# Which groups share the slots of an image, and over how many partitions its transfers run, in a fused group norm, quantised grouped convolution and residual kernel

## What is computed

```
v = group_norm(x, 32 norm groups of 16 channels)          # per image
xg = v by 4 conv groups of 128 channels; output group g reads input group (g + 1) mod 4
xa = round(clip((xg - lA) / (uA - lA), 0, 1) * 15) / 15    # 16 levels
wq = the same for the weights, then (wq - 0.5) * 2         # [4, 128, 128]
y  = per group: wq @ xa                                    # 128 x 128 by 128 x 784
y  = relu(y * inv + (beta - running_mean * inv)),  inv = gamma / sqrt(running_var + eps)
out = x + (y + v)
```

## Time and profile before

| what | us |
|---|---|
| median of 3 runs (317.69 to 323.72) | 322.63 |
| the profiled execution | 316.4 |
| its span | 314.7 |
| busy: PE, DVE, ACT, POOL | 203.8, 232.7, 213.9, 217.8 |
| mean DMA rate over the span | 329 GB/s |
| mean granted TensorE clock | 0.907 of full |

### The profile page before, as it was taken

The page is one execution under the profiler, slowest core; times in us unless marked ns, Lnnn a source line. Parts: engine busy times, 40 slices in busy tenths (PEclk is TensorE's granted clock), DMA queues, the critical chain, the costliest instruction groups (busy, mean ns, idle before and its releaser), DMA issues.

```text
span 314.7 us, 8243 instructions
## 1 busy us (share of the span) xinstructions
PE 203.8 (65%) x3336; PEld 141.0 (45%) x3336; DVE 232.7 (74%) x364; ACT 213.9 (68%) x394; POOL 217.8 (69%) x376
## 2 busy tenths in 40 slices
PE   1122397668586767877777777776858676875640
PEld 0022265455364545455545554554536354643430
DVE  1763567797988979697879897969798796957650
ACT  2222768878797878768797988796978859477000
POOL 5104287787979797959797989797887959696000
PEclk9999999797989989597979997979898698979995
DMA  7999999999999999999999999999999988899987
GB/s 173 231 222 216 215 216 217 270 344 362 398 398 398 398 397 402 401 399 401 395 404 408 411 412 414 408 419 408 409 404 406 404 258 196 187 254 237 244 201 228
DMA packets 19207, 103.56 MB, mean 329 GB/s; under 512 B 2258, under 2 KB 2530, under 8 KB 19170
## 3 DMA queue, kind: packets, MB, share of 16 engines
q1 hardware_dynamic: 10496, 54.86, 53.4%
q10 hardware_dynamic: 8674, 48.18, 44.1%
HBM read 51.65 MB, written 51.38 MB: 327 GB/s over the span
## 4 chain that ended last, share of the span: by engine, by line
PE 44%; DVE 26%; DMA 12%; issue 10%; SPq 3%; ACT 2%; POOL 0%; DVEq 0%; ACTq 0%; POOLq 0%
PE prod L679 39%; DVE images L539 17%; DMA images<-in_x 12%; DVE stats L517 8%; PE mean_ps L638 4%; SPq L222 2%; SPq L234 1%; ACT levels L310 1%; DVE sums L525 1%; ACT unused L274 1%; DVE codes L532 0%; SPq L226 0%; ACT unused L282 0%; DVEq L98 0%; PE var_ps L651 0%
## 5 line engine op out<-in xcount | busy, mean ns | idle before, releaser
L679 PE MATMUL prod<-codes,w_t 64*64 64x392 bf16 x3072 | 165.8, 370 | 51.5 <-DVE images L539 51.5
L539 DVE SCALAR_TENSOR_TENSOR images<-prod,floor,images 128x784 f32<-128x784 f32 x128 | 126.3, 1028 | 50.4 <-PE prod L679 50.3
L679 PEld LDWEIGHTS prod<-codes,w_t 64*64 64x64 bf16 x3072 | 105.0, 119 | 101.9 <-issue 39.2
L470 POOL TENSOR_SCALAR images<-images,coef 128x784 f32<-128x784 f32 x122 | 130.1, 1078 | 0.0
L310 ACT ACTIVATE levels<-images,coef 128x784 int16<-128x784 f32 x95 | 91.4, 1028 | 2.2 <-POOL coef L461 2.2
L517 DVE BATCH_NORM_STATS2 stats<-images 128x6 f32<-128x392 f32 x136 | 66.9, 553 | 17.7 <-DMA images<-in_x 17.7
L274 ACT ACTIVATE unused<-images 128x784 bf16<-128x784 f32 x60 | 50.9, 849 | 40.3 <-DMA images<-in_x 35.8
L282 ACT ACTIVATE unused<-images,sums 128x784 bf16<-128x784 f32 x60 | 56.1, 938 | 0.1
L427 POOL TENSOR_TENSOR dev<-stats,gmean 128x16 f32<-128x16 f32 x16 | 3.7, 229 | 50.6 <-ACT gmean L290 50.6
L532 DVE TENSOR_SCALAR codes<-levels 128x3136 bf16<-128x3136 int16 x32 | 34.1, 1064 | 1.4 <-ACT levels L310 1.4
L481 POOL TENSOR_SCALAR levels<-images,coef 128x784 int16<-128x784 f32 x33 | 33.6, 1020 | 0.1
(11 more groups left out here) (71 smaller groups left out, 83.2 us busy)
## 6 DMA issues: line engine op xcount, KB each, us to landing
images<-in_x SPq DMA_DIRECT2D x60, 784.0 KB, 30.2
out<-images ACTq DMA_DIRECT2D x60, 784.0 KB, 12.5
images<-in_x SPq DMA_DIRECT2D x8, 392.0 KB, 8.1
out<-images SPq DMA_DIRECT2D x2, 784.0 KB, 7.4
out<-images SPq DMA_DIRECT2D x8, 196.0 KB, 3.5
w_raw<-in_weight SPq DMA_DIRECT2D x2, 128.0 KB, 7.4
rows<-in_channel_params ACTq DMA_DIRECT2D x1, 8.0 KB, 1.6
limit_row<-in_limits ACTq DMA_DIRECT2D x1, 0.0 KB
```

The source lines that it names most:

```text
L470: nc.gpsimd.tensor_scalar(here, here, coef[:, u % 2, 0, 1, G * j + o:G * j + o + 1], coef[:, u % 2, 1, 1, G * j + o:G * j + o + 1], ALU.mu ...
L539: nc.vector.scalar_tensor_tensor(out=two, in0=prod[:, PSUM_SET[n % 2][g], :, 0:HALF], scalar=floor[:, o:o + 1], in1=two, op0=ALU.max, op1= ...
L679: done = nc.tensor.matmul(prod[outputs, sets[y], h, 0:HALF], w_t[inputs, part, t, s, outputs], codes[inputs, i % 2, 2 * c + s, h * HALF:(h ...
```

## The change

Groups 0 and 2, and 1 and 3, now share the slots: LOW holds groups 0 (`y = 0`) and 1 (`y = 1`), HIGH holds groups 2 and 3. The views of x, out and the weights are cut by `r` (which half of the partitions, group = 2r + y), so that one transfer takes one `y` with all 128 partitions: in HBM 2 pieces, two groups apart, of 64 rows each. Every load is one transfer per `y`, for the weights too. A store is two transfers, the first after three `final` operations, the second after four. The last image has one transfer per slot. Semaphore counts follow.

The PSUM sets now rotate over all images, (4n + g) mod 3, and `multiply` waits for the `final` operation that frees its second set: three of the image before for t = 0, the first of its own for t = 1, for even and odd images alike. In `multiply` the tiles of output set y read input slots 1 - y, LOW and HIGH from different halves of the partitions; before, all tiles of a set read the same half. The sorting of the weights for it takes 8 operations of 64 partitions instead of 4 of 128. The order of work on the engines is the same, written in another way. Cut to the core:

```diff
-PSUM_SET = ((0, 1, 2, 0), (1, 2, 0, 1))
...
-    GROUPS = ((LOW, slice(0, G, G - 1)), (HIGH, slice(1, G - 1)))
+    HALVES = (LOW, HIGH)
 
     def by_pairs(t):
-        return t.rearrange("b (g i t) h w -> b g i (t h w)", g=G, t=2)
+        return t.rearrange("b (r y i t) h w -> b y r i (t h w)", r=2, y=2, t=2)
 
     x_v, out_v = by_pairs(x), by_pairs(out)
-    w_v = weight.rearrange("(g i t) c -> g i (t c)", g=G, t=2)
+    w_v = weight.rearrange("(r y i t) c -> y r i (t c)", r=2, y=2, t=2)
...
         def store_image(engine, n):
-            engine.wait_ge(final, G * n + G)
-            for part, groups in GROUPS:
-                engine.dma_start(out_v[n, groups].rearrange("y i f -> i y f"),
-                                 pairs_of(images[part, n % RING])).then_inc(stored[n % RING], DMA)
+
+            for y in range(2):
+                engine.wait_ge(final, G * n + 3 + y)
+                engine.dma_start(out_v[n, y], pairs_of(images[:, n % RING])[:, y]).then_inc(stored[n % RING], DMA)
...
-                for part, groups in GROUPS:
-                    sync.dma_start(pairs_of(images[part, j]),
-                                   x_v[n, groups].rearrange("y i f -> i y f")).then_inc(x_loaded[j], DMA)
+                for y in range(2):
+                    sync.dma_start(pairs_of(images[:, j])[:, y], x_v[n, y]).then_inc(x_loaded[j], DMA)
...
-                for part, groups in GROUPS:
-                    sync.dma_start(out_v[B - 1, groups][y][:, t * HW:(t + 1) * HW],
-                                   images[part, j, ORDER[k]]).then_inc(stored[j], DMA)
+                sync.dma_start(out_v[B - 1, y][:, :, t * HW:(t + 1) * HW],
+                               images[:, j, ORDER[k]]).then_inc(stored[j], DMA)
...
-                nc.vector.scalar_tensor_tensor(out=two, in0=prod[:, PSUM_SET[n % 2][g], :, 0:HALF], scalar=floor[:, o:o + 1],
+                nc.vector.scalar_tensor_tensor(out=two, in0=prod[:, (G * n + g) % SETS, :, 0:HALF], scalar=floor[:, o:o + 1],
...
-                done = nc.vector.tensor_scalar(w_sorted[:, g % 2, :, 1 - g // 2], w_rest[:, g].rearrange("p (i s) -> p s i", s=2),
-                                               bn[:, 3, g:g + 1], None, ALU.mult)
+                y, t = g // 2, g % 2
+                for part, inputs in ((LOW, y), (HIGH, 1 - y)):
+                    done = nc.vector.tensor_scalar(w_sorted[part, t, :, inputs],
+                                                   w_rest[part, g].rearrange("p (i s) -> p s i", s=2),
+                                                   bn[part, 3, g:g + 1], None, ALU.mult)
...
-            def multiply(trip, i, t):
-                n, sets = BODY * trip + i, PSUM_SET[i % 2][2 * t:2 * t + 2]
+            def multiply(n, t):
+                first = G * n + 2 * t
                 if t == 0:
                     pe.wait_ge(capped, n + 1)
-                if i > 0 or t == 1:
-                    pe.wait_ge(final, G * n + 1 if t == 1 else G * n - i % 2)
+                if first >= SETS - 1:
+                    pe.wait_ge(final, first + 2 - SETS)
...
-                            for y, inputs in ((0, HIGH), (1, LOW)):
-                                for c, outputs in enumerate((LOW, HIGH)):
-                                    done = nc.tensor.matmul(prod[outputs, sets[y], h, 0:HALF], w_t[inputs, part, t, s, outputs],
-                                                            codes[inputs, i % 2, 2 * c + s, h * HALF:(h + 1) * HALF],
+                            for y in range(2):
+                                for r, outputs in enumerate(HALVES):
+                                    inputs = HALVES[(r + y) % 2]
+                                    done = nc.tensor.matmul(prod[outputs, (first + y) % SETS, h, 0:HALF],
+                                                            w_t[inputs, part, t, s, outputs],
+                                                            codes[inputs, n % 2, 2 * (1 - y) + s, h * HALF:(h + 1) * HALF],
```

More of the change, by code:

```diff
@@ L206, in wait_image @@
             if n < SINGLE:
-                engine.wait_ge(first_loaded[n][g // 2], 2 * DMA)
+                engine.wait_ge(first_loaded[n][g // 2], DMA)
             else:
@@ L220, in _ @@
                 for y in range(2):
-                    for part, groups in GROUPS:
-                        sync.dma_start(pairs_of(images[part, n])[:, y],
-                                       x_v[n, groups][y]).then_inc(first_loaded[n][y], DMA)
+                    sync.dma_start(pairs_of(images[:, n])[:, y], x_v[n, y]).then_inc(first_loaded[n][y], DMA)
                 if n == 0:
-                    for part, groups in GROUPS:
-                        sync.dma_start(pairs_of(w_raw[part]),
-                                       w_v[groups].rearrange("y i f -> i y f")).then_inc(weights_in, DMA)
+                    for y in range(2):
+                        sync.dma_start(pairs_of(w_raw[:])[:, y], w_v[y]).then_inc(weights_in, DMA)
             def load(n):
@@ L244, in _ @@
                 sync.wait_ge(final, G * (B - 1) + k + 1)
-                for part, groups in GROUPS:
-                    sync.dma_start(out_v[B - 1, groups][y][:, t * HW:(t + 1) * HW],
-                                   images[part, j, ORDER[k]]).then_inc(stored[j], DMA)
+                sync.dma_start(out_v[B - 1, y][:, :, t * HW:(t + 1) * HW],
+                               images[:, j, ORDER[k]]).then_inc(stored[j], DMA)
             for j in range(RING):
-                stores = len(range(j, B, RING)) + (G - 1 if j == (B - 1) % RING else 0)
-                sync.wait_ge(stored[j], 2 * DMA * stores)
+                stores = 2 * len(range(j, B, RING)) + (G - 2 if j == (B - 1) % RING else 0)
+                sync.wait_ge(stored[j], DMA * stores)
         @block.scalar
@@ L640, in average_means, with average_deviations @@
                 done.then_inc(mean_done, 1)
[L642 to L643 removed]
+            def average_deviations(u):
                 pe.wait_ge(dev_done, u + 1)
[L645 removed]
+                if u >= 1:
                     pe.wait_ge(std_done, u)
@@ L675, in multiply @@
                             if (part, s, h) == (PARTS - 1, 1, 1):
[L676 to L680 removed]
+                                wait_affines(n, t)
+                            for y in range(2):
+                                for r, outputs in enumerate(HALVES):
[3 more added lines that the diff above has]
+                                                            codes[inputs, n % 2, 2 * (1 - y) + s, h * HALF:(h + 1) * HALF],
                                                             start=(part == 0 and s == 0), stop=(part == PARTS - 1 and s == 1))
                 done.then_inc(multiplied, 1)
[L684 to L690, removed]
             pe.wait_ge(w_scaled, 1)
@@ L696, in _ @@
             turned.then_inc(w_turned, 1)
-            average_means(0, 0)
-            average_deviations(0, 0)
+            average_means(0)
+            average_deviations(0)
             pe.wait_ge(w_ready, 1)
[L700 to L711, removed]
+            average_means(1)
+            for n in range(B):
+                u = n // 2 + 1
+                if n % 2 == 0 and n and u < PAIRS:
+                    average_deviations(u)
+                multiply(n, 0)
+                if n == 0:
+                    average_deviations(1)
+                if n % 2 == 1 and u + 1 < PAIRS:
+                    average_means(u + 1)
+                multiply(n, 1)
 _LIMITS = ["L0_conv_lW", "L0_conv_uW", "L0_conv_lA", "L0_conv_uA"]
```

25 lines of the change are left out of this document (10 added, 15 removed).

## The result

The changed kernel takes 1947.58 us (median of 4 runs, 1947.18 to 1947.69). The kernel before takes 322.17 us beside it (median of 4, 317.69 to 323.72). The ratio is 6.086, with a 95% interval of 6.036 to 6.135. The profiled execution of the changed kernel took 1947.63 us, and 1.7 us of it lie around its span.

A forecast was written before the change was run, and what follows sets the result against it. Two DMA engines at 52.0 GB/s were taken to bound the changed kernel: 1976 us for images, 5 for weights, 2 and 3 at start and end, 1986, with 1.7 around the span 1988, called 1990 us; range 1900 to 2340.

The forecast's parts named there:

- How many engines: Image transfers: outermost counts of 2 and 128 give two DMA engines, 282 packets under 512 bytes; chance 0.86.
- The rate of one engine: Image transfers: 26.0 GB/s for each DMA engine, 52.0 for two, so 1976 us for 32 images both ways.
- The lower bound of 13.6 GB/s with one queue: Stretches of loads or stores alone: each of two engines at only 13.6 GB/s, from 217 / 16 before.
- the high end of 2330: Two engines, slower with one queue: six images of loads and six of stores at 27.2 GB/s, 709 us not 371.
- The start and the pace: First L539 operation at about 163 us and not 42.7, then an image every 62 us.
- Rotation of the sets: Multiply of even images waits for one final less: 0 to 0.85 us for each of 15, some 13; here 0.
- The tile order: Products: even at twice 2.18 us for 48, four groups are 17 us of 61.8, hidden under transfers: 0.
- The half-image stores: First half stored after three final operations: 0 to -1 us per image, counted 0.
- The sorting of the weights: Eight operations, not four of 0.9 us in all: 0 to 1.1 us more, once, during image 1's wait; counted 0.
- The two that kept sixteen engines at a similar or better time: Rivals on transfers: 16 engines, mixed rate also for loads alone, 279 us (0.09); single queue stays at 217 GB/s, 308 to 316 (0.02).
- The 279 us that I gave it: Rival of 16 faster engines: 316.4 less 10 at the start, 23 in the pairs, 4 at the end; chance 0.09.
- The one of slow products: Rival on TensorE: 16 engines, but 48 products take about 4.3 us and not 2.18, some 395 us; chance 0.03.

The follow-up runs named there:

- p1: No computation, transfers alone in 16 forms (pieces in HBM, halves or whole, one or two queues), output copied input: 869.36 us in all.
- e2: The kernel before with the product sets rotating over all images as the only edit: 308.57 us, ratio 0.960.
- e1: The changed kernel with only its transfers undone, each cut by half of the partitions again: 305.47 us, ratio 0.954.
- e7: e1 with each half of an image stored early, in two transfers of 64 partitions, four per image: 304.39 us.
- e6: e5 with its stores changed likewise: y = 0 as one 128-partition transfer after three final operations, y = 1 as two of 64: 297.21 us.
- e5: e2 with groups 0 and 1 loaded as one piece of 128 partitions, groups 3 and 2 still two transfers: 301.60 us.

## Why the prediction was right, and where it was not

**How many engines.** Right, and it was the step that decided. It came from counting completion packets before. Those showed outermost counts of 64, 16 and 1; the step to 2 was argued, not read, and the count of 282 that it named is what the page shows. p1 shows the same for 4 and 8 pieces by the share. The rule of the Trainium skill, "DMA: Bandwidth & Descriptors", section "Why a DMA increments its semaphore by 16 and not by 1", gives 2, 4 and 8 for these cases, and the traces agree (0.13, 0.25, 0.50); it gives 16 for sixteen pieces, and there the trace agrees with the count (0.98) but shows that the rate is not the full one.

**The rate of one engine.** The mis-sized term: 26.0 GB/s, measured 53 / 2 = 26.5. With it the 1976 us for the images become 1939, and the span 1949 for a measured 1945.9. The lower bound of 13.6 GB/s with one queue fell, and with it the high end of 2330: loads alone and stores alone go at 53 like the rest. It came from the earlier trace rows, where 16 engines all wrote to 64 partitions; the two engines of this kernel give the same 53 with one queue at work as with both.

**The start and the pace.** First L532 at 162.80, predicted 163. From image 14's first L532 (950.10) to image 18's (1191.7) it is 60.4 us for an image, predicted 62.

**TensorE.** I said under 13% busy for every compute engine; PE had 15%. Its 203.8 busy us became 287.3, since it idles between images and the granted clock of the middle is 0.53, close to the lower of its two levels. Of 63 product groups that its timeline shows whole, 50 took over 2.5 us, most of them 3.5 to 4.1. It cost nothing here, under transfers of 60 us.

**ScalarE.** Missed: I counted 6.7 us of its own work for an image and idle time ended by DMA. I did not count that its queue stands in the issue of a store, some 30 us at a time, and 655.7 us of its idle time before L267 ended that way. It cost nothing either, since the rate stayed at 53 or 54 GB/s.

**The other edits.** Rotation of the sets: 13.5 us in e2, for the 13 that I named for the case that TensorE and VectorE set the pace. Part of it comes by way of the clock, which the 0.85 us for each even image did not hold, so that the numbers meet is partly luck. The tile order: nothing (e1). The half-image stores: nothing (e7). The sorting of the weights took 2.3 us and not 0.9, 1.4 more, a little over my 1.1, since eight of 282 ns stand one behind the other:

```profile
L573 DVE TENSOR_SCALAR w_raw<-w_rest,bn 64x128 f32<-64x128 f32 x8 | 2.3, 282 | 0.1
```

**The rivals.** The two that kept sixteen engines at a similar or better time fell with the count. Their inner questions were settled apart from it: the half rate belongs to transfers of 64 partitions (p1), as the first of them had it and as the Trainium skill says in "SBUF — State Buffer", section "Door 1: The DMA port swizzle" (some 218 GB/s of it, 206 to 250 here). The 279 us that I gave it are not tested: e6, which moves only half of the bytes in one piece of 128 rows and has the rotation too, is at 297, and no run moves all of them so. The one of slow products, after "TensorEngine Tiling (Array Packing)", section "Restrictions and Gotchas" of the Trainium skill, doesn't come about: pairs of tiles from different partition halves into one set take 2.18 us for 48 products in e1.

## What to carry to other kernels

Before a transfer is made wider in SBUF, look at the outermost count on its HBM side: 2 there meant two DMA engines and 53 GB/s, whatever the 128 partitions could take. Where the data rows are longer than that, the packets under 512 bytes, divided by the number of transfers, tell from a profile how many engines each one gets. If neighbours in HBM are put on the two halves of the partitions, one piece of 128 rows gives 392 to 419 GB/s from a single queue. Half of the loads in that form gained 7 us here by the medians (e5 against e2), in a kernel whose start waits for loads alone.

## What was not expected of the hardware

- Sixteen pieces of 8 rows keep all 16 engines busy (0.98) and load at 231 GB/s, where one piece of 128 rows loads at 392. Eight pieces give 180, under 8 x 26.5 = 212.
- The same two halves on two queues load at 259 GB/s but store at 360; on one queue, in turns, it is 230 and 250.
- One direction in two pieces costs more than half of what both cost: 1155 and 1125 us, where half of 1947 would be 974. The two engines carry their share of the other direction too, and nothing moves it to the 14 that are free. That sum gives 1141 us for the first; single engines are not seen.
- The issue of a DMA can hold its queue: 29.62 us for one store on ScalarE's queue, where it took 0.65 in the kernel before.
